# Masks of the transposed scores: one more key tile of the first head cleared on VectorE instead of masked on TensorE

## The reference, cut to what matters

```python
q, k, v = (proj(Wq), proj(Wk), proj(Wv))          # (B, 16, 512, 16)
scores = jnp.einsum('bhsd,bhtd->bhst', q, k) * scale
scores = jnp.where(mask[None, None, :, :], -jnp.inf, scores)
attn = jax.nn.softmax(scores, axis=-1)
out = jnp.einsum('bhst,bhtd->bhsd', attn, v)
```

## Time and profile before

| | us |
|---|---|
| runs | 1189.94, 1195.78, 1192.04 |
| median | 1192.04 |
| profiled execution, its own time | 1187.42 |
| span in its trace | 1185.7 |
| TensorE busy | 1139.1 |
| VectorE busy | 817.9 |
| ScalarE busy | 736.1 |
| GpSimd busy | 523.4 |

### The profile page before, as it was taken

The page is one execution under the profiler, slowest core; times in us unless marked ns, Lnnn a source line. Parts: engine busy times, 40 slices in busy tenths (PEclk is TensorE's granted clock), DMA queues, the critical chain, the costliest instruction groups (busy, mean ns, idle before and its releaser), DMA issues.

```text
span 1185.7 us, 23441 instructions
## 1 busy us (share of the span) xinstructions
PE 1139.1 (96%) x7525; PEld 772.4 (65%) x7582; DVE 817.9 (69%) x2327; ACT 736.1 (62%) x1628; POOL 523.4 (44%) x837
## 2 busy tenths in 40 slices
PE   7899999999999999999888999999999999999988
PEld 4333433434434344342324999989999999999978
DVE  3889879787897888877783444346555555577647
ACT  2367666676666666666566766655666666666645
POOL 7414226484674755837563457346322222323220
PEclk8899999999999999999899999999999999999999
DMA  8564636648267382663645687936664774823536
GB/s 217 154 215 146 208 123 193 195 163 249 93 214 228 132 248 96 211 198 116 212 158 171 188 292 255 365 68 143 196 198 134 223 229 127 270 48 61 168 89 213
DMA packets 101616, 213.65 MB, mean 180 GB/s; under 512 B 10917, under 2 KB 71341, under 8 KB 93046
## 3 DMA queue, kind: packets, MB, share of 16 engines
q1 hardware_dynamic: 86038, 192.42, 49.7%
q0 software_dynamic: 14304, 18.69, 8.8%
q10 hardware_dynamic: 1152, 1.05, 0.4%
HBM read 239.28 MB, written 74.29 MB: 264 GB/s over the span
## 4 chain that ended last, share of the span: by engine, by line
PE 81%; issue 5%; DVE 4%; ACT 4%; POOL 3%; DMA 2%; another core or an unknown queue 0%; ACTq 0%; DVEq 0%; POOLq 0%
PE bank L1067 38%; PE bank L1168 8%; PE bank L1137 8%; PE bank L1149 7%; PE bank L1153 5%; PE bank L1113 4%; PE bank L1186 2%; PE bank L1121 2%; DVE junk L1602 2%; ACT pt L1334 1%; DMA x<-yout,rows 1%; PE bank L1226 1%; PE bank L1082 1%; PE bank L1206 1%; ACT squared L1282 1%
## 5 line engine op out<-in xcount | busy, mean ns | idle before, releaser
L1602 DVE CUSTOM_DVE_ANT_0 junk<-bank,mneg 128x512 bf16<-128x512 f32 x512 | 335.6, 683 | 93.1 <-PE bank L1137 92.5
L1334 ACT ACTIVATE pt<-bank 128x512 f32<-128x512 f32 x512 | 302.1, 596 | 155.8 <-PE bank L1153 106.8
L1949 POOL DMA_INDIRECT x<-yout,rows x78 | 122.9, 1575 | 289.7 <-ACT yout L1412 241.7
L1067 PE MATMUL bank<-hid,w 128*128 128x256 f32 x1872 | 244.1, 287 | 2.9 <-DVE hid L1750 2.9
L1067 PEld LDWEIGHTS bank<-hid,w 128*128 128x128 f32 x1872 | 230.8, 191 | 4.3 <-ACT full L1407 4.0
L1750 DVE TENSOR_TENSOR hid<-full,hid 128x256 fp32r<-128x256 f32 x312 | 134.4, 435 | 141.2 <-ACT full L1407 139.3
L1402 ACT ACTIVATE hid<-bank,biases 128x256 fp32r<-128x256 f32 x312 | 149.9, 481 | 96.4 <-PE bank L1067 95.2
L1153 PE MATMUL bank<-mneg,identb 128*128 128x512 bf16 x391 | 150.2, 384 | 0.0
L1407 ACT ACTIVATE full<-bank,biases 128x256 f32<-128x256 f32 x312 | 149.2, 478 | 0.0
L1168 PE MATMUL bank<-pt,vaug 128*17 128x512 f32 x1024 | 123.0, 598 | 0.7
L1067 PE MATMUL bank<-rowsT,w 128*128 128x256 f32 x936 | 122.8, 284 | 0.7 <-issue 0.7
(11 more groups left out here) (183 smaller groups left out, 1468.6 us busy)
## 6 DMA issues: line engine op xcount, KB each, us to landing
w<-split_weights SPq DMA_DIRECT2D x80, 1024.0 KB
w<-split_weights SPq DMA_DIRECT2D x40, 2048.0 KB
split_weights<-w_parts SPq DMA_DIRECT2D x64, 512.0 KB, 3.8
w_parts<-in_W SPq DMA_DIRECT2D x64, 256.0 KB, 4.5
split_parts<-parts SPq DMA_DIRECT2D x28, 384.0 KB, 2.6
rows<-routed SPq DMA_DIRECT2D x39, 258.0 KB, 3.4
stacks<-split_parts SPq DMA_DIRECT2D x36, 256.0 KB, 5.4
qst<-split_parts SPq DMA_DIRECT2D x24, 256.0 KB, 5.2
```

Source lines behind the costliest of these rows:

```text
L1067: product = T.matmul(ps, w[p], x[q], start=(k == 0 and n == 0), stop=(k == len(weights) - 1 and n == 2))
L1334: A.activation(pt[n % len(pt)][:, :], bank[3 + n % 2][:, :], ACT.Exp, scale=float(D) ** -0.5).then_inc(exped.sem, 1)
L1602: V.tensor_tensor_reduce(junk[n % 2][:, :], bank[n % 3][:, :], mneg[:, 0, st, :], 1.0, FLOOR, ALU.add, ALU.max, rowmax[gi % 2][:, hh, st:s ...
L1949: G.indirect_dma_start(x2_dram, bass.IndirectOffsetOnAxis(ap=rows[j % NS][:, tt, E + 1:E + 2].bitcast(U32), axis=0), yout[j % NY][:, tt], ...
```

## The change

In the order, the step `clear` of the first head is issued in quarters 0, 1 and 2 rather than 0 and 2. The column step looks the head and tile up in the clears (`limit = (gi, kt, hh) in cleared.value`) and leaves the masking product out where there is one. The weighing waits for the clear of each key tile that has one.

```diff
@@ -297,7 +297,7 @@
                 if 0 <= i - 2 < GROUPS:
                     out.append(("col", i - 2, k, n))
-                    if k % 2 == 0 and n == 2:
+                    if k < ST - 1 and n == 2:
                         out.append(("clear", i - 2, k, 0))
@@ -1161,7 +1161,7 @@
                 pe.wait_ge(*exped.at((gi, kt - kt % 2 + 1, GH - 1)))
-                if kt % 2 == 0:
+                if (gi, kt, 0) in cleared.value:
                     pe.wait_ge(*cleared.at((gi, kt, 0)))
```

## The result

The changed kernel takes 1202.04 us (median of 5, 1201.41 to 1204.14) against 1193.92 us of the kernel before on the same chip (1189.94 to 1195.78): a ratio of 1.008, 95% interval 1.0063 to 1.0096, so 8 us slower by the medians (9.5 by the ratio, which is not that of the two medians and can differ from it by 1 us). I had forecast no change, 1192.0, with a range to 1197.5; the time lies outside.

What follows compares the result with a forecast made beforehand. TensorE was taken to set the pace. Per batch -0.10 - 0 + 0.15 - 0.06 = -0.01 us, eight batches -0.1, ends -0.1: profiled run 1187.4 to 1187.2, so an unchanged median of 1192.0 us, range 1187 to 1197.5.

Steps and rivals of the forecast that it cites:

- What bounds the kernel: Attention stage: TensorE sets the pace on average; row maxima idle 92.5 us and exponentials 106.8 us behind it.
- What TensorE gets: Quarter 1 of each round: a removed masking product is worth 0.22 us by spacing, of which only part comes back.
- position 0: First round of each repeating four: 0.10 us gained on TensorE, no cost from the late row maximum.
- I take 0.61 to 0.64 as its price: VectorE, quarter 1: each added clear delays the row maximum behind it by 0.61 to 0.64 us.
- rival (b): Quarters 1 and 2: GpSimd lengthens clears, the fourth row maximum is late, TensorE waits; 9.7 us in all, 1201.7; chance 0.12.
- Position 1, "Hidden under ScalarE": Second round of four, quarter 2: row score's delay hidden by a column score held 0.50 us by an exponential; cost 0.
- Position 2, 0.15 us: Third round of four, quarter 2: the third row score waits for the late fourth row maximum; cost 0.15 us.
- Position 3, "I cost it at nothing": Fourth round of four: the row maximum ends over a microsecond before its row score; no cost, 0.06 us gained.
- The ends: Around 540 to 567 us a GpSimd chain absorbs clears or gains; last rounds gain 0 to 0.1 us per quarter.
- rival (c): Attention stage: shifted gaps add or remove half-clock stretches of TensorE, 2 to 4 us either way, 1188 or 1196; chance 0.10.
- The signs: Changed profile: 96 clears, VectorE busy up 20 to 26 us, TensorE's waits up 1 to 2, batch same to 0.2.
- The chance of 0.88 for "same": Whole kernel: chance that the time stays within about 0.5% (6 us), against faster 0.05 and slower 0.07.

Runs made afterwards that it cites:

- e1: Kernel before with the first head's second key tile neither masked nor cleared: 1188.7 us against 1193.75, ratio 0.9962.
- e6: Changed kernel with the new clear only in rounds at positions 0 and 2, the masking product kept elsewhere: 1195.66 us, ratio 1.0019 to the kernel before.
- e3: Changed kernel with its 32 new clears made one-input transposes in place: 1191.32 us against 1193.75 of the kernel before, ratio 0.9978.
- e13: Kernel before with key tile 3's mask added to the first head's second key tile, same instructions: 1188.27 us against 1192.74, ratio 0.9966.

## Why the prediction was wrong

- **What bounds the kernel**: right on average, and it misled. VectorE kept 82.9 us of idle time and still cost 9.3 us more of TensorE's waits.
- **What TensorE gets**: right in kind. The spacing (0.22 us) was the measure, not the duration, and only part came back: 0.25 to 0.40 us a batch in e1, where I had 0.16. By TensorE's cut position 0 gives 0.18 against my 0.10 and position 3, without clears, 0.16 against my 0.06. None of it reached the first expert product.
- **"I take 0.61 to 0.64 as its price"**: the step that failed most. It held for the median clear. At position 1 the clear takes 1.62 us in the four rounds 13, 17, 21 and 25, because of where GpSimd's line 1807 stands, and the cast of line 1612 ahead of it takes 1.30 to 1.48 us, held by the same line. The 1678 ns in the earlier trace rows were on the page; I gave rival (b) 0.12 because half the clears of before were short. But which clear is long depends on the place, and I never read what GpSimd does in the place where the new one goes. Rival (b) gave 1201.7 us and 1202.04 came, but that agreement is luck: its sum has 0.39 us a batch at position 1 and 0.82 at position 2, over eight batches; measured (TensorE's cut) are 1.55, with the clock's share, and -0.09, with 0.44 at position 3, and the rounds before 12 lose nothing. Its mechanism, the late fourth maximum behind a blocked clear, is what was found.
- **Position 1, "Hidden under ScalarE"**: wrong. The delay was 0.94 us over the price taken, on top of a cast that was late by 0.5 us; the round is 1.96 us longer (1.55 by TensorE's cut), against 0.
- **Position 2, 0.15 us**: 0.74 in e6, without clears at positions 1 and 3. In the change it is nothing by TensorE's cut (-0.09); the 0.50 us by which it is shorter in the first table is the place of the cut. How it depends on the other positions is open.
- **Position 3, "I cost it at nothing"**: wrong by 0.56 us a batch (0.44 by TensorE's cut). I followed the row maxima behind the clear and not the other instruction behind it, the routing's maximum, although GpSimd and ScalarE wait for it.
- **The ends**: right that they absorb. In e1, round 29 starts 2.8 us earlier than before, and the first expert product only 0.1 us. Part of that is the clock, which in e1 is at its lower level for 10.2 us from 563 us on and before for 6.8 from 566.
- **The clock**: rival (c) had a part. The mean of the whole run hardly shows it (0.987 and 0.983), but the change has two stretches of 3.4 us at the lower level, in rounds 25 and 28, that before has not, behind TensorE's new waits; about 3.2 us of the 9.5, in the range of 2 to 4 us that (c) named.
- **The signs**: 96 clears and 21.6 us more on VectorE came as named. TensorE's waits for row maxima rose by 9.3 us and not by 1 to 2, at position 1 and not 2. The period of a batch rose by 1.8 us, over the 0.4 named, with clears of over 1 us: the sign of (b).
- The chance of 0.88 for "same" rested on four positions read by hand from one batch with exact slacks of 0.1 to 0.5 us. The durations put against them were those of short instructions; the slacks themselves were not tested alone.

## What to carry to other kernels

Before moving work to an engine with idle time, look at the very place where the instruction will stand: what the engine that shares its SBUF port does there, and every instruction behind it, including small ones, with those who wait for them. Look at the instructions ahead of it too: here a cast already held up made the long clear cost more than twice as much. Compare rounds at the engine that sets the pace, and look at the granted clock of each round and not at its mean. Idle time in the sum is no cover; the same 32 clears cost 8 us in one place and nothing behind the next row maximum. A kernel that leaves out part of the computation needs a control with the same instructions and other data.

## What was not expected of the hardware

- Two SBUF inputs or one made about 6.5 of 8 us (an estimate, see e3): the same 32 places took clears of 645 to 1677 ns with two inputs and transposes of 666 to 711 ns with one.
- Other data with the same instructions changed the time by 0.34% (e13), about the size of the effects studied here.
- One wait of 1.55 us on TensorE was followed by 3.4 us at half the granted clock, in which 16 products took 3.45 us instead of 1.91; three other waits of 1.54 us, in rounds 13, 17 and 21, were not.
